# Softmax loop: TensorE computes the remainders ahead of the first transposes of its step

## What is computed

```
attn = jnp.einsum('bhnd,bhmd->bhnm', q, k) * attn_scale
attn, s_attn = fq_act(attn)
...
x_int = x / scale
x_int = x_int - x_int.max(axis=-1, keepdims=True)
q = jnp.floor(x_int / x0_int)
r = x_int - x0_int * q
z = r * (r + b_int) + c_int
exp_int = jnp.clip(jnp.floor(z * jnp.exp2(n - q)), 0.0, None)
exp_sum = exp_int.sum(axis=-1, keepdims=True)
sm = jnp.round(exp_sum / exp_int)
...
o = jnp.einsum('bhnm,bhmd->bhnd', attn, v)
```

## Time and profile before

| | us |
|---|---|
| median of 3 runs | 1104.68 (1103.25 to 1106.07) |
| the profiled execution | 1102.56 |
| its span in the trace | 1100.8 |
| softmax loop, from the first scores to the first issue of the big loads | 440.2 to 634.3 |
| its tail, SyncE's last DMAs and the sums that wait for them | 634.3 to 667 |
| experts | 797.8 to 1100.8 |

### The profile page before, as it was taken

One profiled execution on the slowest core, in us unless ns is written; L12 is line 12 of the kernel. 1 busy time (PEld: TensorE's weight loads), 2 busy tenths in 40 slices (PEclk: granted clock), 3 DMA queues, 4 the chain that ended last, 5 costly groups with the idle time before them and its releaser, 6 DMA issues.

```text
span 1100.8 us, 25924 instructions
## 1 busy us (share of the span) xinstructions
PE 793.8 (72%) x8748; PEld 614.7 (56%) x8748; DVE 804.4 (73%) x1835; ACT 524.3 (48%) x1069; POOL 364.3 (33%) x362
## 2 busy tenths in 40 slices
PE   3699894257716771689999942306199999999998
PEld 2698894246504451355655531205177777777777
DVE  3334551689977997788888876997667777777776
ACT  3122340234436441377777752438245555555554
POOL 2120000368812210122223211000066666666665
PEclk9999897576765555555555555555589999999999
DMA  7942621200003220122222270000000000000000
GB/s 191 267 118 65 189 97 53 87 6 1 0 0 87 69 78 10 39 38 38 44 38 43 39 242 5 9 0 1 10 16 24 25 22 30 15 30 23 22 25 19
DMA packets 114144, 58.14 MB, mean 53 GB/s; under 512 B 75656, under 2 KB 107568, under 8 KB 113968
## 3 DMA queue, kind: packets, MB, share of 16 engines
q1 hardware_dynamic: 112768, 51.24, 18.3%
q0 software_dynamic: 1328, 6.30, 2.0%
HBM read 29.61 MB, written 9.83 MB: 36 GB/s over the span
## 4 chain that ended last, share of the span: by engine, by line
PE 50%; DVE 17%; issue 12%; ACT 8%; SPq 6%; DMA 4%; POOL 2%; DVEq 0%; POOLq 0%; ACTq 0%
PE ps L1389 43%; ACT R L630 5%; PE ps L1551 4%; SPq L500 2%; DMA R<-h_rows 2%; DVE M L1089 2%; DVE M L1090 2%; SPq L472 2%; ACT ps L743 2%; PE ps L1463 1%; DVE R L1285 1%; DVE R L1079 1%; ACT R L633 1%; DVE R L1179 1%; PE ps L1414 1%
## 5 line engine op out<-in xcount | busy, mean ns | idle before, releaser
L1389 PE MATMUL ps<-R 128*128 128x192 f16 (+8 forms) x3618 | 463.3, 281 | 29.5 <-DVE R L895 12.9
L1389 PEld LDWEIGHTS ps<-R 128*128 128x128 f16 (+4 forms) x3618 | 351.3, 115 | 116.7 <-issue 55.8
L622 POOL TENSOR_TENSOR R<-R 128x256 f32<-128x256 f32 x238 | 195.5, 828 | 189.5 <-DVE R L1366 188.0
L1389 PE MATMUL ps<-M 32*64 32x68 bf16 (+2 forms) x2048 | 124.5, 248 | 70.1 <-DMA M<-R 52.4
L1366 DVE TENSOR_TENSOR R<-R,ps 64x256 f32<-64x256 f32 (+1 forms) x272 | 114.0, 419 | 63.5 <-ACT R L838 44.3
L838 ACT ACTIVATE R<-ps 128x256 f32<-128x256 f32 x238 | 91.3, 384 | 137.0 <-PE ps L1389 129.9
L1389 PEld LDWEIGHTS ps<-M 32*64 32x64 bf16 (+2 forms) x2048 | 82.4, 133 | 125.9 <-issue 68.5
L630 ACT ACTIVATE R<-ps 68x896 bf16<-68x896 bf16 (+7 forms) x140 | 94.7, 679 | 118.8 <-PE ps L1463 44.1
L630 ACT ACTIVATE R<-R 128x256 f16<-128x256 f32 (+5 forms) x281 | 125.5, 448 | 22.2 <-POOL R L568 19.8
L1373 DVE TENSOR_TENSOR R<-R 128x256 f16<-128x256 f32 x238 | 113.0, 476 | 20.1 <-ACT R L630 18.0
L633 ACT ACTIVATE R<-R,sc 64x512 f16<-64x512 f32 (+12 forms) x106 | 82.8, 838 | 93.8 <-POOL R L585 41.2
(11 more groups left out here) (234 smaller groups left out, 998.2 us busy)
## 6 DMA issues: line engine op xcount, KB each, us to landing
R<-in_x_dram SPq DMA_DIRECT2D x12, 576.0 KB, 9.7
M<-R SPq DMA_DIRECT2D x16, 260.0 KB, 2.4
M<-R SPq DMA_DIRECT2D x32, 130.0 KB, 2.0
R<-h_rows SPq DMA_DIRECT2D x4, 816.0 KB
R<-h_rows SPq DMA_DIRECT2D x1, 3264.0 KB, 12.8
R<-R SPq DMA_DIRECT2D x17, 192.0 KB, 2.5
out_dram<-R SPq DMA_DIRECT2D x17, 192.0 KB, 2.0
R<-w_split SPq DMA_DIRECT2D x1, 3072.0 KB, 20.6
```

The source lines that it names most:

```text
L622: pool.tensor_tensor(hs[0:rows, m % HB, :], hr[0:rows, m % HB, :], other, ALU.mult).then_inc(sem("squared"), 1)
L1389: return pe.matmul(o, a, b, start=start, stop=stop, skip_group_check=True)
```

## The change

One list is reordered: `remainders` stands first on TensorE's list, `turn_first` second. The same instructions with the same semaphores are issued; nothing else differs, and the queues of the four other engines are the same row for row.

```
-            pipeline(pe, [(turn_first, 4), (remainders, 1), (second_scores, 0), (turn_second, 4), (sum_v, 5)], 32)
+            pipeline(pe, [(remainders, 1), (turn_first, 4), (second_scores, 0), (turn_second, 4), (sum_v, 5)], 32)
```

## The result

| | before | after |
|---|---|---|
| median | 1105.27 (4 runs, 1103.25 to 1106.07) | 1122.14 (4 runs, 1121.43 to 1130.03) |
| the profiled execution | 1102.56 | 1121.43 |
| its span | 1100.8 | 1119.6 |

The changed kernel is slower: ratio 1.0174, 95% interval 1.0133 to 1.0215. Run again later it gave 1122.73 us against 1101.96 of the kernel before beside it, ratio 1.0171, interval 1.0139 to 1.0204. The forecast was 1123, in a range of 1116 to 1128.

A forecast was written before the change was run, and what follows sets the result against it. No engine was full; a loop step of 6.257 us, shared by TensorE and VectorE, was to become 6.93 because transposes delay the scores. Over 26 steps the sum is 18.9 us: 1104.68 + 18.9 = 1123.6, forecast 1123, range 1116 to 1128.

The forecast's parts named there:

- The ring: TensorE's remainders, first transposes, scores, then VectorE's distances to quotients, and remainders again: 6.93 us a step against 6.257.
- The split: On TensorE, remainders take 1.59 us and first transposes 0.77, so scores start 2.36 us after the remainders.
- The gain: Remainders going first on TensorE: at most 0.07 us a step gained, for 27 steps (4 to 30).
- Cover: In the longer step VectorE idles some 0.6 us before distances, TensorE 1.0; no other engine comes near 6.9.
- The end: Step 30's sum_v ends at 649.3 against 630.4, 18.9 us later; SyncE's tail of 36.7 us keeps its length.
- The clock: TensorE in the loop: every group at 1.2 GHz, the one short rise in six steps expected to be lost.
- A (no difference): Rival: within 0.3%, needing some 0.7 us of slack in front of distances; 1103 to 1106; 4%.
- B (clock up and stays): Rival: TensorE's clock comes up and stays in the loop, 13 us less, 1092; 6%.
- C (more rises): Rival: TensorE's clock up in 5 to 15 of 27 steps, each shortened by 0.5 us: 1116 to 1121; 15%.
- D (more than the ring): Rival: switches between TensorE's groups cost 0.25 us each, or a copy comes late: 1129 to 1133; 6%.

The follow-up runs named there:

- the straight line from 1 to 7 transposes: Changed kernel with 1 or 4 first transposes in place of 7: 1107.29 and 1115.51 us; loops 198.06 and 206.22 us, against 214.28 with 7.
- the filled kernel: Changed kernel with 8 empty matmuls in TensorE's pause ahead of the remainders of each step: 1117.79 us, ratio 1.0119.
- the bank behind sum_v: Changed kernel with TensorE's order remainders, scores, first transposes, sum_v, second transposes; sum_v waits for ScalarE to empty its bank (L776): 1135.49 us.
- fourteen transposes: Changed kernel with the seven first transposes done twice, 14 between remainders and scores: 1135.87 us, ratio 1.028.
- the last kernel with the scores ahead of the transposes: Changed kernel reordered to remainders, scores, first transposes, sum_v, second transposes, with ScalarE emptying sum_v's bank before the first transposes' copy: 1121.90 us.

## Why the prediction was right

**The ring.** It was put at 6.93 us a step. From the remainders of step 4 (462.90) to those of step 30 (644.04) the trace has 26 steps, 6.967 each. The parts: remainders to scores 2.36 expected, 562.49 - 560.16 = 2.33 measured; scores to distances 2.11 against 564.64 - 562.49 = 2.15; distances' start to the quotients' end 2.40 against (566.50 + 0.51) - 564.64 = 2.37; to the remainders 0.06 and 0.06. Every second step is 0.17 longer (7.08 against 6.91). The step ahead of the one shown is such a one: 559.52 + 0.51 - 557.57 = 2.46 from distances to quotients, and 0.13 more to the remainders at 560.16. The 2.40 held a part of that, the 0.06 nothing of it. The program's own loop takes two steps per turn, which would fit; no run tests it.

**The split.** Inside the 2.33 the transposes start 1.45 after the remainders and the scores 0.88 after them, where 1.59 and 0.77 were put; that the two errors nearly cancel is luck.

**The gain.** It was put at 0.07 us in every step at most. It came in every second step only: in the others the remainders start 0.13 after the quotients, as in the step shown of before. The ring was reckoned with the 0.06 in all of them, 0.035 us a step too little on average, and it was 6.967 against 6.93.

**Cover.** VectorE's wait ahead of distances was put at some 0.6 us (0.64), TensorE's pause at some 1.0 (1.05 and 1.22). ScalarE, GpSimd and SyncE hold nothing up that they didn't before: no engine waits for one of them by a pair that is new in the stretch from 486 to 630 us.

**The end.** The sum of step 30 was put at an end of 649.3 and ended at 649.89; the last sum near 686, and it started at 686.70. The tail of 36.7 us kept its length (36.81). To the end of that sum the loop is thus 649.89 - 630.43 = 19.46 us later, where 18.9 was put. That the span came out at 18.8 is in part luck: the loop grew by 19.66, but in this execution it began 0.33 us earlier and all behind the last sum was 0.77 us shorter.

**The clock.** The rise was expected to be lost; of five in the loop before one was left, and the loop's mean is 0.51. The 1.6 us worked out for it above is part of the 18.9 already, since the 6.257 of before held its rises.

**The rivals.** A (no difference) needed slack ahead of distances; the straight line from 1 to 7 transposes shows that there is none beyond what one transpose takes. B (clock up and stays) didn't come: with TensorE busy for 187.13 of 209.03 us the filled kernel still had 0.61, and its loop stayed 14.4 us above before. C (more rises) didn't come, with one rise in place of five, and D (more than the ring) didn't either, with a step 0.04 us over the ring.

The Trainium skill, "TensorE: Matmul & The Clock Gate", section "Why this matters for your kernels", asks for a TensorE that is kept busy. In direction the runs agree: filling the pause took the clock from 0.51 to 0.61. In size they don't: with TensorE busy for 187.13 of 209.03 us the clock was 0.61, far from full, and it paid 5 us of 19.7.

## What to carry to other kernels

When a step is moved to the head of a queue, ask first what it pushes back, and look in the trace for who waits for that: here 0.07 us a step stood to be won at the head, half of it came, and 0.06 us was all that the scores had to spare in the step read. An engine's pause is room only if it lies ahead of the thing that others wait for; 1.05 us of pause a step hid nothing. And before a group is moved past another, list every semaphore that it waits for in the other engines' queue order, not only the one in mind, as the bank behind sum_v showed.

## What the runs showed of the hardware

Busy share and granted clock of TensorE didn't go together in these loops. TensorE was busy for 88% of the loop before at a mean clock of 0.54, for 78% with fourteen transposes at 0.63, and for 86% at 0.50 in the last kernel with the scores ahead of the transposes (177.70 of 207.46 us). A part of that is the clock's own effect, since the same matmuls take less time where it is up (1.49 us for the scores against 1.99). Empty matmuls of 128x128 weights raised it each time: 0.51 to 0.61 in the changed kernel, 0.54 to 0.58 and to 0.61 in the kernel before. Why, no run here tells.

The loop begins at times that differ by up to 12.2 us between executions with the same code ahead of it (437.85 to 450.05), while the loop of the changed kernel, profiled twice, repeated within 0.33 us.
